# GpSimd's outer products ahead of the second normalisation, and the state passed on in one transfer

## What is computed

```python
w1 = (x_prev @ w1w.T).reshape(B, T, H, 4); w2 = (x @ w2w.T).reshape(B, T, H, 4)
write_lines = exterior(w1, w2)          # 6 components, divided by their norm
r1, r2 = ...; read_lines = exterior(r1, r2)
Jw = einsum('bthi,ij->bhtj', write_lines, _J6)
outer = Jw[..., :, None] * Jw[..., None, :]           # 6 x 6 per head and token
M_all = decayed running sum of outer over earlier tokens
rd_M = einsum('bhti,bhtij->bhtj', rd, M_all)
mem_score = (1 - alpha) * sum(rd_M * rd) + alpha * sum(rd_M * rd_M)
```

## Time and profile before

| | us |
|---|---|
| median of 3 runs | 1924.51 (1923.56 to 1925.54) |
| the profiled execution | 1925.14 |
| its span | 1923.4 |
| one tile of the memory stage (1187.19 to 1200.01) | 12.82 |
| DVE busy in that tile | 12.14 |
| PE busy in that tile | 11.61 |
| POOL busy in that tile | 7.98 |

### The profile page before, as it was taken

How to read it: one execution, slowest core, us unless ns; L and a number is a source line. 1 busy time by engine, 2 the same in 40 slices (tenths; PEclk the granted TensorE clock), 3 DMA queues, 4 the chain that set the end, 5 groups by cost and what they waited for, 6 DMA issues and landing times. The chain is left out here.

```text
span 1923.4 us, 61311 instructions
## 1 busy us (share of the span) xinstructions
PE 1856.9 (97%) x22646; PEld 1107.9 (58%) x22646; DVE 1604.4 (83%) x5459; ACT 1490.7 (78%) x4110; POOL 920.7 (48%) x552
## 2 busy tenths in 40 slices
PE   7999999999999989999999999889999999999999
PEld 3777774577775343433344347637777635777754
DVE  5999974899995668999999949979999658999945
ACT  4999994699998362777777764469999847999973
POOL 2788861488882050000000035548888505888820
PEclk8999999999999996999999999999999999999999
DMA  5212130122221041111111000002121201121311
GB/s 178 52 44 50 44 70 6 29 50 45 50 53 39 1 153 36 42 42 42 42 42 42 25 6 3 2 20 50 44 51 44 62 6 36 44 50 44 69 23 44
DMA packets 76522, 85.33 MB, mean 44 GB/s; under 512 B 17423, under 2 KB 51027, under 8 KB 76099
## 3 DMA queue, kind: packets, MB, share of 16 engines
q1 hardware_dynamic: 76031, 81.40, 17.0%
q10 hardware_dynamic: 196, 0.02, 0.0%
HBM read 20.83 MB, written 8.39 MB: 15 GB/s over the span
## 5 line engine op out<-in xcount | busy, mean ns | idle before, releaser
L336 ACT ACTIVATE probs<-probs,negmax 128x128 f32<-128x128 f32 x1024 | 401.8, 402 | 1.6 <-DVE negmax L411 1.0
L2334 ACT ACTIVATE gprobs<-ps_global 128x1024 f32<-128x1024 f32 (+3 forms) x384 | 291.5, 811 | 125.9 <-PE ps_global L1765 103.2
L291 POOL TENSOR_TENSOR rot<-rot 128x1024 f32<-128x1024 f32 x128 | 302.3, 2362 | 144.8 <-DVE rot L381 144.8
L297 POOL TENSOR_TENSOR qk<-rot,cnorm 128x1024 f32<-128x1024 f32 x128 | 243.8, 1905 | 172.8 <-issue 149.0
L304 POOL TENSOR_TENSOR probs<-probs,iden 128x1024 f32<-128x1024 f32 x128 | 242.8, 1897 | 46.6 <-DVE iden L419 46.0
L2010 DVE TENSOR_REDUCE maxes<-ps_global 128x1 f32<-128x512 f32 (+2 forms) x384 | 221.9, 636 | 11.5 <-PE ps_global L1728 6.5
L411 DVE CUSTOM_DVE_ANT_0 probs<-ps_attn,masks 128x128 f32<-128x128 f32 x1024 | 226.0, 284 | 0.6 <-issue 0.5
L1723 PE MATMUL ps_global<-kq 48*128 48x512 bf16 (+3 forms) x768 | 197.4, 346 | 7.0 <-DVE maxes L2010 1.8
L336 ACT ACTIVATION_READ_ACCUMULATOR probs<-probs,negmax 128x1 f32 x1024 | 203.9, 199 | 0.0
L2251 POOL CAST m_parts<-m_turn 32x128 bf16<-32x128 f32 x16 | 4.5, 280 | 364.6 <-DVE m_turn L2024 364.6
L377 DVE TENSOR_TENSOR rot<-ps_attn,rotary 128x512 f32<-128x512 f32 x256 | 174.7, 682 | 3.1 <-PE ps_attn L202 2.6
(11 more groups left out here) (235 smaller groups left out, 4489.7 us busy)
## 6 DMA issues: line engine op xcount, KB each, us to landing
v_first<-v_second SPq DMA_DIRECT2D x256, 128.0 KB, 2.3
hs<-z_a SPq DMA_DIRECT2D x256, 32.0 KB, 1.9
ln<-z_b SPq DMA_DIRECT2D x56, 128.0 KB, 2.4
kq<-split_scratch SPq DMA_DIRECT2D x64, 96.0 KB
kq<-split_scratch SPq DMA_DIRECT2D x64, 64.0 KB
split_scratch<-parts SPq DMA_DIRECT2D x8, 384.0 KB, 4.3
split_scratch<-gprobs SPq DMA_DIRECT2D x6, 384.0 KB, 4.0
x_tok<-in_x_dram SPq DMA_DIRECT2D x4, 512.0 KB, 5.9
```

The costliest lines, as they stand in the source:

```text
L291: nc.gpsimd.tensor_tensor(a, a, b, ALU.add).then_inc(C["rot_sum"], 1)
L297: nc.gpsimd.tensor_tensor(qk[:, k % 2, :].rearrange("p (h d) -> p h d", d=DH), rot_a[:, k % 2, :, :], cnorm[:, k % 2, :].unsqueeze(2).to_b ...
L336: last = nc.scalar.activation(probs[:, k % 2, slot, :], probs[:, k % 2, slot, :], ACT.Exp, scale=-1.0, bias=negmax[:, k % 2, slot:slot + 1 ...
L2334: nc.scalar.activation(probs[:, step % RING, 2 * p:2 * p + 2, 0:w], ps[:, S0 + 2 * p:S0 + 2 * p + 2, 0:w], ACT.Exp).then_inc(C["p2_exp"], 1)
```

## The change

Three things are changed. In POOL's `body(t)`, `normalise(t + 1, 1)` now stands behind `outer_products(t + 1)` at the start of the body, where `normalise(t + 2, 1)` stood at the end of the body before it. So POOL's order becomes `normalise(k, 0)`, `outer_products(k)`, `normalise(k, 1)`. `pass_state(k)` issues one DMA of 4 rows of 2304 bytes, where it issued four of 4 rows of 576 bytes; it can do so because the heads are dealt out to the 4 PE column groups in another order, h = GROUPS * j + q, in `tails`. The waits on `ml_row` count 16 a tile instead of 64, and the four small DMAs of `whole` read 4 neighbouring heads instead of every fourth one. No other engine's order is changed.

```diff
                 for q in range(GROUPS):
                     for j in range(GROUP):
-                        h = GROUP * q + j
+                        h = GROUPS * j + q
...
-                    wait(pe, f"ml_row{k % 2}", 16 * GROUP * (k // 2 + 1))
+                    wait(pe, f"ml_row{k % 2}", 16 * (k // 2 + 1))
...
-                wait(dve, f"ml_row{(k + 1) % 2}", 16 * GROUP * ((k + 1) // 2))
+                wait(dve, f"ml_row{(k + 1) % 2}", 16 * ((k + 1) // 2))
...
             def body(t):
                 if valid(t + 1):
                     outer_products(t + 1)
+                    normalise(t + 1, 1)
                 if valid(t + 2):
                     subtract(t + 2, 0)
                     subtract(t + 2, 1)
                     normalise(t + 2, 0)
-                    normalise(t + 2, 1)
...
-                for j in range(GROUP):
-                    sp.dma_start(outer[TILE - 1:TILE, k % 2, j:AH:GROUP, :], state[32 * j:32 * j + 1, k % 2, :, :]
-                                 ).then_inc(C[f"ml_row{k % 2}"], 16)
+                sp.dma_start(outer[TILE - 1:TILE, k % 2, :, :].rearrange("p (j q) n -> p j (q n)", j=GROUP),
+                             state[0:P:32, k % 2, :, :].rearrange("j q n -> j (q n)")).then_inc(C[f"ml_row{k % 2}"], 16)
...
-            sp.dma_start(A["whole"][32 * j:32 * j + 1, :], decay[0:1, j:AH:GROUP, TILE], allow_slow_non_contiguous=True
+            sp.dma_start(A["whole"][32 * j:32 * j + 1, :], decay[0:1, GROUPS * j:GROUPS * (j + 1), TILE], allow_slow_non_contiguous=True
```

## The result

The changed kernel takes 1952.12 us (median of 4 runs, 1949.06 to 1955.29) against 1924.53: the ratio is 1.0141, with an interval of 1.0129 to 1.0154. It is 27.6 us slower. The forecast was 1944.9 with a range up to 1950.5, so the sign was right and the size too small. Ratios and their intervals are of fast runs alone, which leaves out one run of the kernel before (1972.5) and one of the old order with three more matmuls (2589.5), both at a clearly lower clock. The profiled execution is the longest of the four: 1955.3 us, span 1953.5, 30.1 over the span of before.

A forecast was written before the change was run, and what follows sets the result against it. DVE was taken to bound the memory stage's tile. On the profiled 1925.1 us, terms -1.2 + 17.1 + 1.3 - 0.7 + 3.9 = +20.4, less 0.6, gave 1944.9 us; range 1938.5 to 1950.5.

The forecast's parts named there:

- What bounds the kernel: Memory-stage tile: DVE bounds it, busy 12.14 of 12.82 us; with its wait gone, PE's last projection and ACT's copy come next.
- Part 1: Outer products start 1.5 us earlier; gain 0.29 us a tile in four tiles, 1.2 us (bounds 0 and 2.2).
- Part 2: DVE's second clip is held until POOL's outer products end: 3.42 us in each of tiles 2 to 6, 17.1 us.
- Part 3: Last tile: PE's wait for the state's row goes, 2.15 us, but the held clip adds 3.4; net +1.3 us.
- Part 4: Head: ACT's inverse root of tile 1 no longer waits for DVE, saving 0.7 us (0 to 0.7).
- Part 5: PE idles 4.2 us in held tiles and its clock falls: three of six tiles at 1.3 us, +3.9 (0 to 20).
- the clock falls in most tiles: Rival: PE's clock falls in six tiles at up to 3.4 us each, on 1941.0: 1950 to 1961 us; chance 0.06.
- The clip isn't held: Rival: DVE's one-SBUF-input clip runs beside POOL's outer products without a hold: 1920.4 us; chance 0.12.
- The merged DMA is slow: Rival: the single state DMA's longer rows cost time, only in the last tile, under 0.5 us; no separate chance given.

The follow-up runs named there:

- the old order with three more matmuls: POOL's old order with the one state transfer and three extra 128x512 matmuls filling PE's waits: 1921.22 us, ratio 0.9983 to the kernel before.
- The clip against PSUM: Changed kernel with the second clip of tiles 2 to 7 done as a minimum with a constant in PSUM: 1924.33 us, ratio 0.9988.
- the reduction: Changed kernel with the second clip of tiles 2 to 7 written as an SBUF-to-SBUF reduction, without the upper limit: 1921.89 us, ratio 0.9982.
- four pieces: Changed kernel with the outer products as four POOL instructions of 4 heads each instead of one: 1928.65 us, ratio 1.0018.
- the kernel with PE kept busy: Changed kernel with three unread 128x512 matmuls in the middle of PE's body in tiles 2 to 7: 1941.18 us, ratio 1.0072.
- the outer products behind the clip: Changed kernel with one more POOL wait, so the outer products start after the tile's second clip: 1925.21 us, ratio 0.9993.
- the merge alone: The state's one transfer and the new head order, on POOL's old order: 1923.78 us, ratio 0.9986 to the kernel before.
- the kernel with two matmuls more: Changed kernel with its second clip taken against a PSUM constant, plus two 128x512 matmuls on PE ahead of the last tile's terms: 1921.66 us, ratio 0.9973.

## Why the prediction missed its range

- **What bounds the kernel: right.** The clip against PSUM and the reduction give tiles of 12.54 us, with PE's projection and ACT's copy as the next bound.
- **Part 1: right.** 0.28 us a tile (12.82 to 12.54) where 0.29 stood; over tiles 2 to 6 the kernel with the reduction takes 63.06 against 64.18, 1.1 us, where 1.2 stood. Between a first clip and the start of the outer products are 1.20 us instead of 2.74, the 1.5 of the forecast.
- **Part 2: right, to 0.02 us.** Clips of 3.62 against 0.18 us, 3.44 a tile. Tile 1 is spared (0.19). In tile 0 the clip lasts 2.85 us and costs nothing, as costed: the head is 0.70 us shorter in spite of it, and just as long (29.89 us) with four pieces, where this clip lasts 1.07. The evidence from other instructions (L399, L2070, L527) carried over.
- **Part 3: right where it could be seen.** The merge saves 1.65 us in the last tile when alone (19.28 to 17.63 from its first clip to the first scaling, L2110), and with the earlier outer products and the clock at 1.00 it saves 2.21 (17.07), where 1.8 and 2.15 stood. No run has the last tile with a held clip and the clock at 1.00, so the +1.3 as a whole wasn't measured.
- **Part 4: right.** 0.70 us (30.59 to 29.89 between the first clips of tiles 0 and 2).
- **Part 5: the step that failed, in count and in size.** I took the clock to fall in three of six tiles at 1.3 us each, 3.9 us. It fell in all six, behind idle times of 4.6 to 6.0 us where I had put 4.2. Against the tiles of the kernel with PE kept busy, the five cost 18.76 - 15.95, 18.14 - 16.35, 17.40 - 15.95, 17.24 - 15.95 and 18.83 - 15.95, that is 2.8, 1.8, 1.45, 1.3 and 2.9, in all 10.2 us; the last tile, with part 3's own 1.3 taken off, cost 43.41 - 40.26 - 1.3 = 1.9. That is 12.1 us, 2.0 a tile. By the medians it is 1952.1 - 1941.2 = 10.9, but the kernel with PE kept busy has a fall of its own in the last tile (2.6 - 1.3 = 1.3), and with it the two agree. The price of 1.3 was right for the two tiles that were slow for 3.4 us; the four that were slow for 6.8 us cost 1.8 to 2.9. With 11 to 12 in place of 3.9 the sum gives 1952 to 1953.
- **The rival that held** is "the clock falls in most tiles", which had 0.06. What I had set against it was that PE is busy for 12 of 16 us, so the clock has time to come back. It does come back in each tile, and that protects none of the next: it falls again at the next hold. The slack that I counted on took a part of the slow stretches, but not enough: half of their length is 17.1 us, of which 12.1 reached the time. PE's items, ACT's copies and DVE's multiplications stand in a row, and the 14.2 us that DVE waited for L2375 (4.5 before) are where it surfaced. Two stretches in the earlier trace rows, one of 2.31 us without a fall and one of 3.83 with one, were taken as if a stretch beyond both could be spared half of the time. That left the upper end at 1950.5, between bounds of 0 and 20 us that the text itself had named.
- **"The clip isn't held": refuted** for this form of the instruction, and its time of 1920.4 is about what the kernel takes whose clip is not held: 1921.9, with one fall of the clock in its last tile.
- **"The merged DMA is slow": refuted.** One issue of 0.50 us for four in 2.40, and the wait behind it is shorter by 1.65.

What stays open: which tile's idle time makes the clock fall. Ahead of the last tile's products, idle times of 2.54 us (the reduction), 2.55 (the clip against PSUM), 2.89 (the outer products behind the clip) and 3.08 (four pieces) were followed by a fall, and 2.31 (before) and 2.81 (the merge alone) were not. I only know what was read after the fact.

## What to carry to other kernels

Before a small instruction of VectorE is left to fall beside a long one of GpSimd, look at its form: here a tensor_scalar of 64 elements from SBUF to SBUF was held until GpSimd's present instruction ended (3.62 us), while a reduction (0.21 us) and a form with one operand in PSUM (0.22 us) were not. Changing the form removed the hold, and cutting the long instruction shortened it. Price a hold by more than its length: if TensorE idles for it, add the half clock behind it, here 2 us on top of 3.4. The clock fell in six of six tiles with 4.6 us or more of idle time, in four of five with 2.7 to 3.1, and in none of five with 1.7 to 2.1. And where the clock falls in a wait, work whose result nobody reads can make the kernel faster if it lies inside that wait (11 us here); put in front of TensorE's own work it was simply work (tiles of 24 us).

## What the runs showed of the hardware beyond that

- POOL doesn't keep DVE held from one instruction to the next: with four pieces back to back, DVE's clip got through behind the first (0.74 us).
- Cutting the outer products in pieces costs little: four of 1.15 us follow each other at 1.10, 4.4 us for 4.03.
- The clock can also fall behind short waits close together, though not each time: in the last tile of the kernel with two matmuls more, behind waits of 1.09, 0.48 and 0.35 us, it was at 0.50 for some 3.4 us, and behind the same three waits in the kernel with the reduction it stayed at 1.00; one matmul of 1.02 us in the first of these waits kept it at 1.00, and the rest of the stage was 1.4 us shorter.
